# Attention on 96 padded rows: stacks filled by transfers within SBUF, the maximum's row sent by ACT

## The reference

```python
x = x + _L1_attn_ref(_layernorm(x), ...)

def _L1_attn_ref(x, ocr_context, Wq, bq, Wk, bk, Wv, bv, Wo, bo, ocr_bias):
    # D_MODEL 256, N_HEADS 16, HEAD_DIM 16
    q = x @ Wq.T + bq + ocr_bias
    k = x @ Wk.T + bk
    v = x @ Wv.T + bv
    ...
    scores = jnp.einsum('bhsd,bhtd->bhst', q, k) / math.sqrt(HEAD_DIM)
    scores = scores + _band_mask(S, scores.dtype)
    attn = jax.nn.softmax(scores, axis=-1)
    out = jnp.einsum('bhst,bhtd->bhsd', attn, v)
    out = out.transpose(0, 2, 1, 3).reshape(B, S, D_MODEL)
    return out @ Wo.T + bo
```

## Time and profile before

| | |
|---|---|
| median of 3 runs | 4211.57 us (4206.95 to 4215.46) |
| profiled execution | 4213.35 us, its span 4211.6 us |
| mean granted TensorE clock | 0.957 of full speed |
| busy: PE, DVE, ACT, POOL | 89%, 65%, 43%, 32% of the span |
| attention stage | from about 2108 to 3460 us of the span |

### The profile page before, as it was taken

The page is one execution under the profiler, slowest core; times in us unless marked ns, Lnnn a source line. Parts: engine busy times, 40 slices in busy tenths (PEclk is TensorE's granted clock), DMA queues, the critical chain, the costliest instruction groups (busy, mean ns, idle before and its releaser), DMA issues. The chain is left out here.

```text
span 4211.6 us, 79961 instructions
## 1 busy us (share of the span) xinstructions
PE 3768.9 (89%) x27516; PEld 2923.9 (69%) x27516; DVE 2720.6 (65%) x5626; ACT 1790.0 (43%) x3205; POOL 1364.4 (32%) x1045
## 2 busy tenths in 40 slices
PE   6997888887997999999968899998999979999999
PEld 4886677776886888888734455554555538888888
DVE  5665677775676566666655666666676655666665
ACT  3444344443554333333325555555555553333333
POOL 2555222222665222222222323323323322222222
PEclk9998999998998999999969999999999989999999
DMA  3000000000001000000034334333333410000000
GB/s 101 0 0 14 2 0 0 0 0 1 0 0 38 1 0 0 0 0 0 10 69 90 76 67 90 83 68 86 86 68 83 90 46 6 15 10 10 15 10 16
DMA packets 72273, 131.72 MB, mean 31 GB/s; under 512 B 7776, under 2 KB 40944, under 8 KB 66048
## 3 DMA queue, kind: packets, MB, share of 16 engines
q1 hardware_dynamic: 72192, 130.65, 13.2%
HBM read 71.38 MB, written 58.72 MB: 31 GB/s over the span
## 5 line engine op out<-in xcount | busy, mean ns | idle before, releaser
L1476 DVE TENSOR_REDUCE neg_max_sb<-s_ps 128x1 f32<-128x512 f32 x1024 | 689.5, 687 | 436.0 <-PE s_ps L1217 433.1
L1382 ACT ACTIVATE prob_sb<-s_ps 128x512 f32<-128x512 f32 x1024 | 599.8, 599 | 543.4 <-PE s_ps L1229 532.7
L850 POOL TENSOR_TENSOR m_act_lo_sb<-m_act_sb,m_act_hi_sb 128x512 fp32r<-128x512 f32 x320 | 414.1, 1294 | 1042.1 <-ACT m_act_hi_sb L816 1042.1
L806 ACT ACTIVATE m_silu_sb<-moe_h_ps 128x512 f32<-128x512 f32 x320 | 191.4, 598 | 966.7 <-PE moe_h_ps L761 966.7
L1229 PE MATMUL s_ps<-q_stack_sb,k_stack_sb 97*128 97x512 f32 x1024 | 483.3, 473 | 101.5 <-DMA q_stack_sb<-neg_max_t_sb 87.2
L1134 POOL TENSOR_TENSOR prob_sb<-prob_sb,band_sb 128x520 f32<-128x520 f32 (+1 forms) x256 | 285.2, 1114 | 853.0 <-ACT prob_sb L1382 852.9
L904 DVE TENSOR_TENSOR m_act_sb<-moe_h_ps,m_silu_sb 128x512 f32<-128x512 f32 x320 | 220.6, 689 | 502.1 <-ACT m_silu_sb L806 472.4
L1229 PEld LDWEIGHTS s_ps<-q_stack_sb,k_stack_sb 97*128 97x128 f32 x1024 | 203.0, 199 | 409.4 <-ACT prob_sb L1382 239.1
L1217 PE MATMUL s_ps<-k_stack_sb,q_stack_sb 96*128 96x512 f32 x1024 | 451.8, 444 | 28.7 <-DMA k_stack_sb<-qk_scratch 16.3
L529 POOL TENSOR_TENSOR f_sq_lo_sb<-f_sq_sb,f_sq_hi_sb 128x512 fp32r<-128x512 f32 x256 | 329.6, 1296 | 349.8 <-ACT f_sq_hi_sb L504 349.7
L916 DVE SCALAR_TENSOR_TENSOR x_resident_sb<-moe_y_ps,gates_sb,x_resident_sb 128x256 f32 (+1 forms) x1024 | 422.5, 474 | 0.5
(11 more groups left out here) (282 smaller groups left out, 8904.4 us busy)
## 6 DMA issues: line engine op xcount, KB each, us to landing
qk_scratch<-qk_hi_sb SPq DMA_DIRECT2D x128, 256.0 KB
q_stack_sb<-qk_scratch SPq DMA_DIRECT2D x64, 384.0 KB, 5.2
k_stack_sb<-qk_scratch SPq DMA_DIRECT2D x64, 384.0 KB, 7.0
qk_scratch<-qk_lo_sb SPq DMA_DIRECT2D x64, 256.0 KB
x_resident_sb<-x SPq DMA_DIRECT2D x4, 2048.0 KB, 17.8
out<-x_resident_sb SPq DMA_DIRECT2D x16, 512.0 KB, 2.9
moe_w_values_sb<-routed_w SPq DMA_DIRECT2D x12, 512.0 KB, 6.5
moe_w_values_sb<-shared_w SPq DMA_DIRECT2D x6, 256.0 KB, 5.4
```

Of the source, the lines that this page charges most:

```text
L850: nc.gpsimd.tensor_tensor(al[:, slot(e), :], act_f[:, e % 2, :], as_f32(ah[:, slot(e), :]), ALU.subtract).then_inc(low_ready, 1)
L1382: nc.scalar.activation(prob[:, kt % 2, i, :], s2p[i % 2][:, :], ACT.Exp).then_inc(exp_done, 1)
L1476: nc.vector.tensor_reduce(nm[:, g % 2, i, qt:qt + 1], s1p[i % 2][:, :], AXIS_X, ALU.max, negate=True).then_inc(max_done, 1)
```

## The change

It removes the DRAM scratch. SP now copies from `qk_hi` and `qk_lo` straight to the stacks, one transfer for each head and slot of 16 partitions x 512 elements (32 KB): 16 for the high and 8 for the low part of a group, 96 a sequence (`to_stacks`). A group's transfers wait until the second products of that group in the sequence before have run (`s2_ready`), as the loads did. `low_part` and `high_part` for m = 1 now wait until the transfers of groups 0 and 1 have landed (`q_loaded`, `k_loaded`), those of the next m = 0 for groups 2 and 3. The row of the maximum is sent from ACT's queue, right after ACT's copy, for which ACT waits. In the new code the lines of `att_stage` have other numbers; the transfers are line 1064, the row line 1367.

```diff
-        scratch = nc.dram_tensor("qk_scratch", (KT, 2, 3, HD, HEADS // KT, TOKENS), F32).ap()
...
-        PER_LOAD, PER_WRITE = 16 * 2, 16 * 6
+        PER_LOAD = 16 * 3 * GH
...
-                def write(b, m, part, ready):
-
+                def to_stacks(b, g, part, ready):
+
+                    m = g // 2
                     sp.wait_ge(ready, KT * b + m + 1)
                     hold(sp, turns)
                     if part == 0 and not first(b):
-                        for g in (2 * m, 2 * m + 1):
-                            sp.wait_ge(loaded[g], PER_LOAD * b)
+                        sp.wait_ge(s2_ready, (b - 1) * STEPS * GH + TILES * GH * (g + 1))
                     src = (qkh, qkl)[part]
...
+                    for i in range(GH):
+                        head = slice(HD * (GH * (g % 2) + i), HD * (GH * (g % 2) + i + 1))
+                        for x, (stack, done) in enumerate(((qs, q_loaded[g]), (ks, k_loaded[g]))):
+                            for slot in (((0, 1), (0, 2)), ((2,), (1,)))[part][x]:
+                                sp.dma_start(as_f32(stack[HD * slot:HD * (slot + 1), g, i, :]),
+                                             as_f32(src[head, x, :])).then_inc(done, 16)
 
                 for m in range(KT):
-                    write(0, m, 0, qkh_ready)
-                    write(0, m, 1, qkl_ready)
-                    load(0, 2 * m)
-                    load(0, 2 * m + 1)
-                max_row(0, 0)
+                    for part, ready in enumerate((qkh_ready, qkl_ready)):
+                        to_stacks(0, 2 * m, part, ready)
+                        to_stacks(0, 2 * m + 1, part, ready)
 
                 def body(b, before, more):
...
+                        for g in range(GROUPS):
+                            to_stacks(b + 1, g, 0, qkh_ready)
+                            to_stacks(b + 1, g, 1, qkl_ready)
...
                     if x == 0:
                         act.wait_ge(full_ready, 2 * (KT * b + m + 1))
-                        if m:
-                            act.wait_ge(written[0], PER_WRITE * b + PER_WRITE)
-                        elif not first(b):
-                            act.wait_ge(written[1], PER_WRITE * b)
+                        for g in (2 * m - 2, 2 * m - 1):
+                            if m or not first(b):
+                                act.wait_ge(q_loaded[g % GROUPS], PER_LOAD * b + PER_LOAD * m)
+                                act.wait_ge(k_loaded[g % GROUPS], PER_LOAD * b + PER_LOAD * m)
...
                     nc.scalar.copy(nmt[:, g % 2, :], mp[0:TILES * GH, 0:P]).then_inc(nmt_ready, 1)
+                    act.wait_ge(nmt_ready, b * GROUPS + g + 1)
+                    act.dma_start(as_f32(qs[MAX_ROW:MAX_ROW + 1, g, :, :]), as_f32(nmt[:, g % 2, :])).then_inc(rowed[g], 16)
```

More of the change, by code:

```diff
@@ L1023, in att_stage @@
         rowed = [s(f"{name}_max_row{g}") for g in range(GROUPS)]
-        loaded = [s(f"{name}_stack{g}") for g in range(GROUPS)]
-        written = [s(f"{name}_written{m}") for m in range(KT)]
+        q_loaded = [s(f"{name}_q_stack{g}") for g in range(GROUPS)]
+        k_loaded = [s(f"{name}_k_stack{g}") for g in range(GROUPS)]
         ot_ready = s(name + "_ot_ready")
@@ L1078, in max_row @@
-                def max_row(b, g):
-                    sp.wait_ge(nmt_ready, b * GROUPS + g + 1)
-                    sp.dma_start(as_f32(qs[MAX_ROW:MAX_ROW + 1, g, :, :]), as_f32(nmt[:, g % 2, :])).then_inc(rowed[g], 16)
-                for m in range(KT):
-                    write(0, m, 0, qkh_ready)
-                    write(0, m, 1, qkl_ready)
-                    load(0, 2 * m)
-                    load(0, 2 * m + 1)
-                max_row(0, 0)
+                    for i in range(GH):
[4 more added lines that the diff above has]
+                                             as_f32(src[head, x, :])).then_inc(done, 16)
@@ L1089, in body @@
+                for m in range(KT):
+                    for part, ready in enumerate((qkh_ready, qkl_ready)):
+                        to_stacks(0, 2 * m, part, ready)
+                        to_stacks(0, 2 * m + 1, part, ready)
                 def body(b, before, more):
-                    max_row(b, 1)
                     if more:
[L1092 to L1104, removed]
+                        for g in range(GROUPS):
+                            to_stacks(b + 1, g, 0, qkh_ready)
+                            to_stacks(b + 1, g, 1, qkl_ready)
                 over_sequences(sp, core.batches, body)
@@ L1138, in low_part @@
                     pool.wait_ge(qkh_ready, KT * b + m + 1)
-                    if m:
-                        pool.wait_ge(written[0], PER_WRITE * b + PER_WRITE)
-                    elif not first(b):
-                        pool.wait_ge(written[1], PER_WRITE * b)
+                    for g in (2 * m - 2, 2 * m - 1):
+                        if m or not first(b):
+                            pool.wait_ge(q_loaded[g % GROUPS], PER_LOAD * b + PER_LOAD * m)
+                            pool.wait_ge(k_loaded[g % GROUPS], PER_LOAD * b + PER_LOAD * m)
                     nc.gpsimd.tensor_tensor(qkl[:, :, :], full[:, :, :], as_f32(qkh[:, :, :]),
@@ L1213, in s1_unit @@
                     if qt == 0 and i == 0:
-                        pe.wait_ge(loaded[g], PER_LOAD * b + PER_LOAD)
+                        pe.wait_ge(q_loaded[g], PER_LOAD * b + PER_LOAD)
+                        pe.wait_ge(k_loaded[g], PER_LOAD * b + PER_LOAD)
                     pe.wait_ge(max_done, (b * STEPS + st) * GH + i + 1)
```

## The result

The changed kernel takes 4328.23 us (median of 4 runs, 4322.78 to 4330.75), the kernel before took 4213.31 in the runs beside it: ratio 1.0274, 95% interval 1.0256 to 1.0291. It is slower by 115 us, outside the range. The profiled execution after took 4326.08 us, its span 4324.4.

What follows compares the result with a forecast made beforehand. PE was taken as the bound, busy 1087 of 1200 us in the attention stage. Removing the old loss (-131 us) and adding the new (+123 us) gave -8 us on 4211.6: 4204 us, practically unchanged, range 4100 to 4290.

Steps and rivals of the forecast that it cites:

- The old loss: PE's two waits a sequence for the maximum's row (steps 8, 12), 85 us, plus low clock, 46 us: 131 us gone.
- The new wait: ACT's cast at step 9 waits for 48 issues on SP; PE then waits 4.6 us at step 10, once a sequence.
- I take 0.46, the nearest row in kind: Price of each stack transfer's issue on SP, 0.46 us, taken from the biases issued back to back.
- issues of 0.52 us and more: Case where group 0's cover is gone: PE waits at step 9 as well, as part of the same delay.
- The transfers pace: Rival: stack transfers of 32 KB take 0.64 us each, PE waits 13.6 us a sequence; 4339 us, chance 0.16.
- Shorter issues: Rival: SP's issues take 0.38 us, PE waits only 0.8 us a sequence; 4102 us, chance 0.14.
- the row not in time: Rival: the maximum's row crosses SP's 96 transfers badly, both old waits stay; 4335 us, called small, rest 0.04.
- The clock, 3.0 us a sequence: Low clock behind PE's new wait, where output projections follow: 6.7 us run low, costing 3.0 us a sequence.
- ACT, 0.6: ACT's four row issues a sequence, 2.8 us, partly hidden in idle time: 0.6 us a sequence reaches PE.
- The prologue, nothing: Ahead of the first step, 40 issues replace six writes and two loads and a 2.2 us wait goes: set to zero.
- Against the rule: A DMA's fixed cost of about 2.0 us, paid in series, would make the chain 96 us; refused because small transfers overlap.

Runs made afterwards that it cites:

- pair_low_act: The changed kernel with slot 0 of q and k filled by one transfer and ACT issuing the low parts of groups 0 and 1: 4097.7 us.
- the two runs above: The kernel before with the maximum's row sent by ACT: 4184.1 us; the kernel before with SP sending rows ahead of the writes: 4166.7 us.
- row_sp_first: The kernel before with only SP's order changed, the rows of groups 2 and 3 ahead of the six writes each: 4166.7 us.
- issue_forms: The changed kernel with other transfer forms in groups 0, 2 and 3 (half the bytes, to DRAM, small from DRAM): 4318.5 us, one run.
- pair_issue: The changed kernel with q's and k's stacks in one tile, slot 0 of both by one transfer, 80 transfers a sequence instead of 96: 4241.9 us.
- low16_on_act: The changed kernel with the 16 low-part transfers of groups 0 and 1 issued by ACT instead of SP: 4153.1 us.

## Why the prediction was wrong

*The old loss, -8.7 us a sequence:* borne out. Without any long wait a sequence takes 72.5 us (pair_low_act); 79.95 - 8.7 is 71.3, and ACT's issues add about one. Taken away alone, though, it uncovers the load of group 0, which the [0.20 us] row of step 9 showed to be due just then.

*The new wait:* right in place and mechanism, the cast at step 9 and PE at step 10 behind it, once a sequence.

**The step that failed** is "I take 0.46, the nearest row in kind" for the issue. The runs showed 0.63 us from issue to issue. In the prediction's own sum, 47 x 0.17 = 8.0 us more make the wait 12.6 us in place of 4.6; measured are 1.9 + 9.9 = 11.8, the first part at step 9, as said for issues of 0.52 us and more. 8.0 x 15 = 120 us, put on 4204, give 4324. That this comes within 4 us of the 4328 is partly luck: the terms below are off as well, in both directions. The prediction had bounded the price by 0.64, but gave that end to the transfers and little chance. The biases were taken because they stand back to back; but they come from DRAM, and have 0.5 KB. The one transfer from SBUF to SBUF in the trace was the row, issue 0.56 us, and I had read it as a price of ACT alone.

*The transfers pace:* its time (4339) was near, its mechanism wrong. The transfers land 2.0 us after their issue by the median and 3.9 at most, the DMA engines are idle 83%, and double or half the bytes hardly change the issue (0.63 and 0.59 us). *Shorter issues* and *the row not in time* were wrong: the cast waits, and PE's list has no row.

*The clock, 3.0 us a sequence:* it is 1.5 to 2.5: most of the low time falls into the wait itself, and 3.5 us of work (above) to 5.7 (2595.5 to 2601.2, another sequence) at the low level lose 44%. *ACT, 0.6:* about 1.1, by the two runs above. *The prologue, nothing:* this too was wrong. The first product came 33.4 us after the first projection (2123.45 to 2156.88), before 26.6 (2126.26 to 2152.83), and in the first sequence PE then waited 6.4 and 3.6 us for groups 1 and 2. With 9.2, 2.2 and 9.8 us at the new places these are 38 us up to the first addition, against 19 of old waits that are gone. The 19 left are most of the 22.6 us by which it is longer from the first projection to the first addition; the projection itself came 2.8 us earlier, which leaves the 20 above. A sequence's account, -8.7 + 11.8 + 2.0 + 1.1 = 6.2 of 7.2 us, leaves 1.0 open.

*Against the rule:* paying 2.0 us per transfer in series was rightly refused: the 48 take 0.636 us each, though each lands about 2.0 us after its issue. (The section that the prediction cites for the 2.0 us is on DMAs issued by GpSimd; these go from SP.) The Trainium skill (Perfetto Trace Analysis, section "What "DMA-bound" means") names the other bound, an issuing engine's queue that is solid with DMA; SP's rows between 2649.96 and 2680.4 show it.

## What to carry to other kernels

Price a chain of small transfers by the issue of a transfer with the same two ends and as many partitions, and multiply before trusting the mean: 48 x 0.17 us turned no change into a loss. When a queue is solid with issues while the DMA engines idle, merge transfers, or share them with a second queue whose engine has idle time beside them; halving their bytes did nothing here. A wait removed is worth what the next one due behind it leaves: row_sp_first kept 45 of 131 us.

## What the runs showed of the hardware

Issues on SP's queue, by the median: with both ends in SBUF 16x256 and 16x512 took 0.59 us and 16x1024 took 0.63 (issue_forms, pair_issue); with one end in DRAM 16x512 (to DRAM) and 16x8 (from DRAM) took 0.42 (issue_forms). 128 partitions to DRAM took 0.64 and 1.44 us (the kernel before). ACT's queue issued the low parts in 0.51 and 0.61 us while ACT computed exponentials (low16_on_act). Why two SBUF ends cost 0.17 us more stays open.
